# A macaron layer on one core: the feed-forward's down projection as products of halves with streamed weights, and norms and routing in pieces among the scan units

## The reference

```
x1 = x  + 0.5 * ffn(layernorm(x))
x2 = x1 + attn(layernorm(x1))
out= x2 + 0.5 * ffn(layernorm(x2))

ffn(x):  scores = sigmoid(x @ gate_w)                      # 32 experts
         top 6 scores, divided by their sum = combine      # zero for the others
         g, u = x @ wg[e], x @ wu[e]                       # 32 x 96 hidden columns
         routed = sum_e combine[e] * (silu(g) * u) @ wd[e]
         shared = (silu(x @ sg) * (x @ su)) @ sd           # 192 hidden columns
attn(x): h = x + mamba(rmsnorm(x));  h + mlp(rmsnorm(h))   # mlp: gate/up/down, 1024 wide
mamba:   in_proj -> z, x, B, C, dt; causal conv of 4 taps, silu; softplus(dt)
         h[t] = exp(dt*A) * h[t-1] + dt*x*B;  y = h . C    # 512 channels x 16 states
         (y + D*x) * silu(z) @ out_proj
```

## Time and profile before

| | us |
|---|---|
| median of 3 runs (lowest, highest) | 1938.59 (1936.56, 1942.36) |
| the profiled execution | 1936.02 |
| its span, first to last instruction | 1934.2 |
| PE / DVE / ACT / POOL busy | 1601.1 / 1295.1 / 705.1 / 720.2 |
| mean granted TensorE clock | 0.934 of full |

### The profile page before, as it was taken

How to read it: one execution, slowest core, us unless ns; L and a number is a source line. 1 busy time by engine, 2 the same in 40 slices (tenths; PEclk the granted TensorE clock), 3 DMA queues, 4 the chain that set the end, 5 groups by cost and what they waited for, 6 DMA issues and landing times. The chain is left out here.

```text
span 1934.2 us, 25234 instructions
## 1 busy us (share of the span) xinstructions
PE 1601.1 (83%) x7512; PEld 1194.2 (62%) x7512; DVE 1295.1 (67%) x2331; ACT 705.1 (36%) x1418; POOL 720.2 (37%) x838
## 2 busy tenths in 40 slices
PE   6776768677978988789888989788988998678999
PEld 5665557555755557455664557555675567556888
DVE  3236984688468964789466974689648974896343
ACT  4234424433352425333343423433244334432211
POOL 4411552244134532345223542245324542353222
PEclk9887889878999999899998999899999999988999
DMA  7752223323232222222231223222232223323563
GB/s 260 281 170 91 86 86 99 111 88 98 78 106 72 81 89 74 105 74 80 80 104 65 84 77 95 85 77 88 81 98 93 87 77 86 126 88 101 174 205 133
DMA packets 72751, 204.77 MB, mean 106 GB/s; under 512 B 12928, under 2 KB 22368, under 8 KB 72224
## 3 DMA queue, kind: packets, MB, share of 16 engines
q1 hardware_dynamic: 64416, 177.86, 27.7%
q0 software_dynamic: 8192, 25.17, 4.5%
HBM read 179.39 MB, written 15.73 MB: 101 GB/s over the span
## 5 line engine op out<-in xcount | busy, mean ns | idle before, releaser
L595 PE MATMUL gub<-x_hi,wr 128*128 128x256 f32 (+1 forms) x1144 | 460.5, 403 | 83.5 <-DVE hid L963 60.6
L675 PE MATMUL acc<-hid,w_down 128*128 128x256 f32 (+1 forms) x1144 | 423.9, 498 | 0.9 <-DVE hid L963 0.8
L1218 POOL TENSOR_TENSOR hid<-hid,weight 128x256 f32<-128x256 f32 (+1 forms) x264 | 263.5, 998 | 428.0 <-DVE hid L963 409.9
L824 ACT ACTIVATE hid<-gub 128x256 f32<-128x256 f32 (+1 forms) x350 | 160.9, 460 | 680.5 <-PE gub L597 590.5
L596 PE MATMUL gub<-x_lo,wr 128*128 128x256 f32 (+1 forms) x1144 | 395.7, 346 | 0.0
L597 PE MATMUL gub<-x_hi,wr 128*128 128x256 f32 (+1 forms) x1144 | 394.7, 345 | 0.0
L1231 POOL TENSOR_TENSOR ring<-ring 128x512 f32<-128x512 f32 x192 | 245.8, 1280 | 314.4 <-DVE ring L1118 314.4
L1112 DVE TENSOR_TENSOR_SCAN ring<-decays,side 128x512 f32<-128x512 f32 x256 | 310.7, 1214 | 4.1 <-DVE side L1103 1.5
L595 PEld LDWEIGHTS gub<-x_hi,wr 128*128 128x128 f32 x1144 | 231.9, 203 | 122.1 <-issue 73.9
L675 PEld LDWEIGHTS acc<-hid,w_down 128*128 128x128 f32 x1144 | 212.9, 201 | 88.3 <-issue 68.8
L596 PEld LDWEIGHTS gub<-x_lo,wr 128*128 128x128 f32 x1144 | 232.3, 203 | 21.1 <-issue 4.3
(11 more groups left out here) (115 smaller groups left out, 1725.4 us busy)
## 6 DMA issues: line engine op xcount, KB each, us to landing
wr<-w_halves SPq DMA_DIRECT2D x260, 512.0 KB, 3.3
wm_gu<-in_w_mlp POOLq DMA_DIRECT2D x64, 256.0 KB, 3.0
w_halves<-wr SPq DMA_DIRECT2D x26, 512.0 KB, 4.9
wm_down<-in_w_mlp POOLq DMA_DIRECT2D x64, 128.0 KB, 2.6
w_raw<-in_w_gu SPq DMA_DIRECT2D x26, 256.0 KB, 4.7
cst<-decays SPq DMA_DIRECT2D x192, 32.0 KB, 1.9
xin<-in_x SPq DMA_DIRECT2D x8, 256.0 KB, 3.4
x<-in_x SPq DMA_DIRECT2D x8, 256.0 KB, 2.6
```

The source lines that it names most:

```text
L595: mm(out, w[:, 0, half, k, :], x_hi[:, k, a:b], start=(k == 0), stop=False)
L675: last = mm(acc[k][:, a:b], w, h[:, a:b], start=(c == 0), stop=(c == (MLP_CHUNKS if mlp else FFN_CHUNKS) - 1))
L824: A(hid[c % HSLOTS][:, a:b], s.gub_of(it)[:, a:b], ACT.Tanh, scale=0.5).then_inc(sem["tanh_done"], 1)
L1218: nc.gpsimd.tensor_tensor(h, h, weight[c // 3 % CSLOTS][:, a:b], ALU.mult).then_inc(sem["weighted"], 1)
```

## The change

Two things. First, the ffn's `down` product is made as gate and up are: `w_hi h_hi + w_hi h_lo + w_lo h_hi`, six fp32r products instead of two f32 ones. A new item `hh` makes h_hi (copy on ScalarE) and h_lo (subtraction on GpSimd) of `hid`. The down weights' halves join those of gate and up: raw loads become 384 KB, halves 768 KB, `w_down` is no longer resident. The split `ws` of w_lo moves from GpSimd to VectorE. A slot is free for its next load only after `down`. `down` stands four chunks behind `g`. Second, `n2` is cut in two (`nm` is its VectorE part) and the route into eight pieces `rq`, each an item of its own in the list.

```diff
+ROUTE = (2, 3, 1, 3, 2, 2, 2, 4)
+    "hh": {"hid_hi": 1, "hid_lo": 1},
+def norm(which):
+    return [("n1", which), ("n2", which), ("nm", which)]
+def routing(call):
+    return [("rt1", call)] + [("rq", call, i) for i in range(len(ROUTE))]
-LENGTH = {"n1": 3, "n2": 5, ... "rt1": 8,
+LENGTH = {"n1": 3, "n2": 3, "nm": 2, "rq": 0.75, ... "rt1": 2,
-SHORT = {"n1": 3, "n2": 8.0, ... "rt1": 8,
+SHORT = {"n1": 3, "n2": 6.0, "nm": 2.0, "rq": 0.75, ... "rt1": 2,
-DLAG = 3
+DLAG = 4
 # ffn_items
+        out += [("hh", "ff", p - 2)] if 2 <= p <= FFN_CHUNKS + 1 else []
         out += [("down", "ff", p - DLAG)] if p >= DLAG else []
         out += [("by_g", "ff", p), ("u", "ff", p)] if now else []
+        used = p - DLAG
-        elif p + WSLOTS < FFN_CHUNKS:
-            out += [("wl", p + WSLOTS)]
-        if now and more and p == last_in(p % WSLOTS):
-            out += [("wln", p % WSLOTS)]
+        elif used >= 0 and used + WSLOTS < FFN_CHUNKS:
+            out += [("wl", used + WSLOTS)]
+        if more and used >= 0 and used == last_in(used % WSLOTS):
+            out += [("wln", used % WSLOTS)]
-LAG = {"n1": 0, "n2": 3, ... "rt1": 3, ...
+LAG = {"n1": 0, "n2": 0, "nm": 3, "rq": 0, ... "rt1": 0, ...
-        w_down = sb("w_down", [P, FFN_CHUNKS, DM])
-        wr = [sb(f"wr{i}", [P, 2, 2, KC, P], F32R) for i in range(WSLOTS)]
+        wr = [sb(f"wr{i}", [P, 2, 3, KC, P], F32R) for i in range(WSLOTS)]
+        h_hi = [sb(f"h_hi{i}", [P, 2 * SEQ], F32R) for i in range(PSLOTS)]
+        h_lo = [sb(f"h_lo{i}", [P, 2 * SEQ], F32R) for i in range(PSLOTS)]
 # SyncE, wl and wln
-                    sp.wait_ge(sem["u_filled"], s.count("u_filled", ("u", "ff", before), 1))
+                    sp.wait_ge(sem["down_done"], s.count("down_done", ("down", "ff", before), 1))
 # TensorE, down of the ffn
+                        pe.wait_ge(sem["hid_lo"], s.count("hid_lo", ("hh", "ff", c), 1))
+                        w = wr[c % WSLOTS]
+                        hi, lo = h_hi[c % PSLOTS][:, a:b], h_lo[c % PSLOTS][:, a:b]
+                        for k in range(KC):
+                            mm(acc[k][:, a:b], w[:, 0, 2, k, :], hi, start=(c == 0), stop=False)
+                            mm(acc[k][:, a:b], w[:, 0, 2, k, :], lo, start=False, stop=False)
+                            last = mm(acc[k][:, a:b], w[:, 1, 2, k, :], hi, start=False,
+                                      stop=(c == FFN_CHUNKS - 1))
 # ScalarE, hh
+                    A(h_hi[c % PSLOTS][:, a:b], hid[c % HSLOTS][:, a:b], ACT.Copy).then_inc(sem["hid_hi"], 1)
 # GpSimd, hh
+                    nc.gpsimd.tensor_tensor(h_lo[c % PSLOTS][:, a:b], hid[c % HSLOTS][:, a:b],
+                                            h_hi[c % PSLOTS][:, a:b].bitcast(F32),
+                                            ALU.subtract).then_inc(sem["hid_lo"], 1)
 # VectorE, ws (was GpSimd's)
+                    v.tensor_tensor(w[:, 1], w_raw[it[1] % RAWS][:], w[:, 0].bitcast(F32),
+                                    ALU.subtract).then_inc(sem["w_split"], 1)
 # VectorE, route: the same instructions, one piece per item
+                if piece == 0:
+                    link(v.tensor_scalar(e_sc[:], e_sc[:], 1.0, None, ALU.add))
+                    settle()
+                    link(v.reciprocal(sc[:, :, 0:E], e_sc[:]))
+                if piece == 1:    # pace, two max
+                elif piece == 2:  # tensor_copy top8 <- marks
+                elif piece == 3:  # pace, two match_replace
+                elif piece == 4:  # subtract, tensor_reduce
+                elif piece == 5:  # tensor_scalar, reciprocal
+                elif piece == 6:  # two tensor_scalar
+                elif piece == 7:  # copy, subtract, copy, subtract
```

More of the change, by code:

```diff
@@ L80 @@
     "n1r": {"squared": 1},
-    "n2c": {"side_filled": 1, "logged": 1, "rstd": 1, "normed": 1},
-    "n2r": {"side_filled": 1, "logged": 1, "rstd": 1, "normed": KC},
-    "rt1": {"side_filled": 1, "rt_exp": 1, "routing": 19},
+    "n2": {"side_filled": 1, "logged": 1, "rstd": 1},
+    "nmc": {"normed": 1},
+    "nmr": {"normed": KC},
+    "rt1": {"side_filled": 1, "rt_exp": 1},
+    **{f"rq{i}": {"routing": links} for i, links in enumerate(ROUTE)},
     "rt2": {"side_filled": 1, "comb_ready": 1},
@@ L134, in items_of @@
     if t < 0:
-        return [("load",), ("n1", "ln1"), ("n2", "ln1"), ("rt1", "f1")]
+        return [("load",)] + norm("ln1") + routing("f1")
     hand = ([("hx", "f1")] if first else []) + ([("hx", "f2")] if second else [])
@@ L139, in items_of @@
     keep += [("load",)] if following else []
-    norms = [("n1", "lnA"), ("n2", "lnA"), ("n1", "rms1"), ("n2", "rms1")] if mamba else []
+    norms = norm("lnA") + norm("rms1") if mamba else []
     project = ([("split", 0), ("x", 0), ("split", 1), ("x", 1), ("z", 0), ("split", 2), ("z", 1),
@@ L143, in items_of @@
     units = [(k, u) for u in range(UNITS) for k in ("ub", "unit")] if mamba else []
-    last = [("yz",), ("outp",), ("n1", "rms2"), ("n2", "rms2")] if mamba else []
+    last = [("yz",), ("outp",)] + norm("rms2") if mamba else []
     r0 = ([("r0",)] if mamba else []) + ([("again",)] if first else [])
-    ln2 = [("n1", "ln2"), ("n2", "ln2"), ("rt1", "f2")] if mlp else []
-    ln1 = [("n1", "ln1"), ("n2", "ln1"), ("rt1", "f1")] if following else []
+    ln2 = norm("ln2") + routing("f2") if mlp else []
+    ln1 = norm("ln1") + routing("f1") if following else []
     ahead = [(k, c) for c in range(MSLOTS) for k in ("mgn", "mdn")] if 0 <= t + 1 - 2 < BATCH else []
@@ L819, in do @@
                     act.wait_ge(sem[filled], s.count(filled, it, 1))
-                    if (least := s.count("down_done", ("down",) + it[1:], 1,
-                                         back=HSLOTS if c >= 2 else 2)) is not None:
-                        act.wait_ge(sem["down_done"], least)
+                    if c >= HSLOTS and kind == "gum":
+                        act.wait_ge(sem["down_done"], s.count("down_done", ("down", "mlp", c - HSLOTS), 1))
+                    elif c >= HSLOTS:
+                        act.wait_ge(sem["hid_lo"], s.count("hid_lo", ("hh", "ff", c - HSLOTS), 1))
+                    elif kind == "g" and ("end", "mlp") in s.at:
+                        act.wait_ge(sem["down_done"], s.count("down_done", ("down", "mlp", MLP_CHUNKS - 1), 1))
+                    elif (least := s.prior("hid_lo")) is not None:
+                        act.wait_ge(sem["hid_lo"], least)
                     A(hid[c % HSLOTS][:, a:b], s.gub_of(it)[:, a:b], ACT.Tanh,
@@ L1002, in do @@
                                         ALU.subtract).then_inc(sem["centered"], 1)
-                elif kind == "n2":
-                    dve.wait_ge(sem["rstd"], s.count("rstd", it, 1))
+                elif kind == "nm":
+                    dve.wait_ge(sem["rstd"], s.count("rstd", ("n2", it[1]), 1))
                     if it[1] in ("rms1", "rms2"):
@@ L1015, in do @@
                         v.tensor_tensor(dst[:], dst[:], twice(rstd[:, :]), ALU.mult).then_inc(sem["normed"], 1)
-                elif kind == "rt1":
+                elif kind == "rq":
                     route(s, it)
@@ L1131, in route @@
             def route(s, it):
+                E = EXPERTS
+                out, piece = c3[it[1]], it[2]
                 done = [0]
@@ L1300 @@
     arrays = {
-        "x": xt, "w_gu": w_gu, "w_down": down, "w_mlp": w_mlp,
+        "x": xt, "w_ffn": w_ffn, "w_mlp": w_mlp,
         "w_router": feat(g["ffn_gate_w"]), "w_in": w_in, "w_dt": c(g["attn_dt_proj_w"].T),
```

164 lines of the change are left out of this document (78 added, 86 removed).

## The result

| | us |
|---|---|
| after, median of 4 runs (lowest, highest) | 1966.49 (1958.60, 1967.64) |
| before, on the same chip, median of 4 runs | 1938.11 |
| ratio after to before, 95% interval | 1.0129 [1.0105, 1.0153] |
| forecast (range) | 1911 (1868 to 1948) |

What follows compares the result with a forecast made beforehand. Scan stretches were taken as set by VectorE plus stalls it starts itself, other parts by TensorE or latency chains. From 1936.0 us, -13 -67 +36 +13 +6 = -25 gave 1911, range 1868 to 1948.

Steps and rivals of the forecast that it cites:

- Down products: Ffn's down products: 1.38 us a chunk instead of 1.72 at 512 columns, paying only at ends of steps: -13 us.
- Halves of hid: ScalarE's copies and GpSimd's subtractions of hid: GpSimd at 97 us in a scan stretch, yet cost 0.
- three ring slots cover: In the scan, three ring slots keep y adds queued behind GpSimd's subtractions from delaying VectorE's units: cost 0.
- rival (b): GpSimd paces the scan, its in-order queue delaying y adds: +45 to +50 us, 1958 us; chance 0.2.
- Norms and routing in pieces: Scan stretches lose 60 of 72 us of VectorE's waits, t=9 another 7: together -67 us.
- collisions (+36): VectorE's norm and routing pieces in scan stretches wait until GpSimd's running instruction ends: +36 us.
- all lengths sum as before: Item lengths of the split norms and routing add up to the old ones, so the units keep their places.
- forecast medians near 0.5: Sign to look for: VectorE's L1144, L1152, L1162 and L1171 would have median durations near 0.5 us.
- Weights, start: t=0 moves more weight data; first product of t=1 near 134 instead of 122.42: +13 us.
- Weights, later: Loads of chunks 0 and 1 go out at a step's end; mlp hides them except in t=10: +6 us.
- Rival (c): Weights late: t=0/1 at +25 us, t=9 and 10 paced by loads: 1936 us, no change; chance 0.12.
- six tails: Ends of six mamba steps, where cheaper down products were counted as 1 us each.

Runs made afterwards that it cites:

- e2: The kernel before with down halves, hh, streamed weights and the lag of 4 alone, norms and routing as blocks: 1959.02 us, ratio 1.008.
- e11: The whole change with four weight loads sent later, routing as one block and GpSimd's subtraction over 64 columns (computation left out): 1903.48 us.
- e8: The kernel before with norms in pieces and routing as one contiguous block, no halves: 1902.19 us.
- e4: The whole change with GpSimd's subtraction for the low half of hid over 64 columns instead of 256 or 512 (computation left out): 1935.64 us.
- e14: The kernel before with the halves alone, norms and routing as blocks, and GpSimd's subtraction over 64 columns (computation left out): 1931.56 us.
- e6: The whole change with four weight loads sent later, four tail items instead of six and GpSimd's subtraction over 64 columns (computation left out): 1922.70 us.
- e1: The kernel before with norms and routing in pieces alone; down products, weights and loads as before: 1910.56 us, ratio 0.9839.
- e12: The kernel before with only ln1, ln2 and rms2 in pieces; lnA, rms1 and routing as blocks, no halves: 1891.85 us, ratio 0.9751.
- e18: The whole change with four weight loads sent later and lnA and rms1 as blocks at their old places: 1917.26 us.
- e9: The whole change, all items in place, with four weight loads per step sent behind mlp products 3 to 6 of the next step: 1948.24 us.
- e13: The kernel before with the halves alone, norms and routing as blocks, and the four loads at the turn of a step sent later: 1923.91 us.
- e10: The whole change with weight loads of 512 KB a chunk instead of 768, the down weights' halves not loaded again (computation wrong): 1947.60 us.

## Why the prediction was wrong, step by step

**Down products (-13).** Price right (1.38 us); what it was worth was not isolated. In e2 the scan stretches are 19 us shorter, against "In scan stretches VectorE is last, so there it buys nothing itself". But e2 also changes the lag and the order, and the waits that shrank are those for rstd (50.6 to 25.7 us). Whether the shorter products or the order brought rstd earlier is open. Beside the pieces this gain is gone: e11, with loads moved and subtractions shortened, has scan stretches of 912.2 us against 908.3 in e8, and ends level with it (-36.8 and -38.7). At the ends of loop steps the price makes 1.4 us (estimate above), near the 1 us that I took.

**Halves of hid (0, "three ring slots cover").** This failed. GpSimd's load in the scan was near the forecast (87 us against 97), and it doesn't pace the scan: no wait of VectorE for the y adds (L1273) stands in the window above, so rival (b) did not come in its own way. But its subtractions cost 29 to 37 us (e4, e14, e6). Where it went is in part argued: VectorE's busy time fell by 28 us in e4, the projections from 244.3 to 234.7, the scan stretches from 912.0 to 903.8. I priced collisions for the pieces and not for the new subtraction. One group of VectorE's, the four y products ahead of the first driven input, is enough to see it (after; 1.56 us at 1006.81 before):

```profile
1029.93 3.21 DVE L1131 TENSOR_SCALAR xs<-xs,vecs 128x256 f32<-128x256 f32 x4
```

**Norms and routing in pieces (-67), collisions (+36).** The net, -31, is what e1 gave, -29, and the scan stretches fell even below the forecast. The parts: routing in pieces stretches by 2.3 us a call in e1 (37 us over 16), as forecast, and by 3.1 in the change. Wrong is that it buys something: as a block (e8) the kernel is 9.7 us faster, with TensorE at full clock. Nearly all of the gain is the norms' in the scan, and the pieces of lnA and rms1 cost 10 (e12) to 30 us (e18), where I had counted "all lengths sum as before" as no cost. In t=9 the pieces gave 3 us in e1, not the 7 of the sum. In the head each of these two is a link of a chain, dts waits for both. The forecast medians near 0.5 were mixed: 0.94, 0.17, 0.96, 0.44.

The rule of the Trainium skill (SBUF — State Buffer, "SBUF: two separate sides"), that GpSimd and VectorE with two SBUF inputs or a two-port mode lock each other out for an instruction, fits the rows above: constant additions and casts go up to 1.2 us, MAX8 stays at 174 to 192 ns. It was the same rule that should have priced the subtraction.

**Weights, start (+13).** Wrong in sign for t=0: 8 us shorter. The first product of t=1 came at 121.06, not 134 (122.42 before), after a stand of 8.63 us on "issue" (2.12 before). t=1 was 11 us longer, 7 of them in x_hi to dts; 3 us net at its end.

**Weights, later (+6).** t=10 came as forecast: its `PE gub L605 <- DMA wr<-w_halves` waits 5.6 us, the step is 5 longer. What failed is the sentence "Steps with mlp first hide it". They hide the weights of chunks 0 and 1, but not the loads themselves: 20 us (e9) to 37 us (e13) came back when they were moved away from the starts of t=1 to 8. There they filled the DMA engines just when the mlp's weights, and as I argue the next instructions, were wanted; part of it is TensorE's clock behind the stands. Beside the subtractions this is the cost that the sum lacked. I asked only who waits for these loads, not what waits behind them. Rival (c), weights late for their own products, was not it.

**The sum.** It said -25 and +28 was measured, a miss of 53. Two terms that it had at nothing make nearly that by medians: the subtractions 32 (e4) and the loads at the turn 20 (e9). That the rest came out near -25 is in part luck, as single terms of it were off (start 3 instead of 13, the routing's pieces a loss of their own, the pieces of lnA and rms1 at no cost). Three slips in the working change little: VectorE's two shorter kinds of wait make 16.1 us, a third (0.4) the 16.5; scan units stand in eight steps, so six tails are 2 us short; 111 and 25 are 136, not 134.

It also took the parts as additive. They are not, by 38 us of medians and 33 in the profiled executions. 21 of the 33 are the scan: pieces alone take 41.5 us off the scan stretches, on top of the halves 20, as both remove the same stands of VectorE (its 50.6 us of waits for rstd are 25.7 with the halves alone, 5.1 with the pieces alone), and the stretch then lies at VectorE's 112 to 116 us plus 6 to 12. Ten lie between gated product and residual, which the pieces shorten by 7 us alone and lengthen by 4 beside the halves, five behind the last scan. How much of these is collisions and how much the order of the items was not separated.

## What to carry to other kernels

Two changes that relieve the same stretch don't add; find what floor remains (here VectorE's busy time) before summing. When a transfer is moved, price what stands behind it on the DMA engines, perhaps the program's own instructions too, and not only its user. When a stretch between two marks changes, count the work in it before calling it won or lost. Splitting work into pieces pays where it fills a wait between independent units and costs where the work is a chain of its own; small two-port VectorE instructions next to a fed GpSimd are best kept together.

## What the runs showed of the hardware that was not expected

- Instructions come over the same DMA engines as data. With the engines 0.99 busy at a loop's turn, TensorE and VectorE stood 3.13 and 4.80 us on nothing shown; with the same loads some 15 to 40 us later, 1.53 and 1.73. That the late instruction packets are the cause was argued from the queue rows; the experiment moved the loads, not the packets. In t=2, with no turn of the loop, TensorE stood 3.17 us the same way.
- A third less in each load (e10) helped as much as moving four of them (21 and 20 us). The stand before x_hi stayed; TensorE's second stand and the half clock behind it shrank.
- A GpSimd subtraction of 64 columns takes 0.37 us, of 256 columns 0.76, of 512 columns 1.35. A VectorE addition of 0.16 us takes up to 1.23 beside such work.
